# Attention scores from two float32r pieces in the two halves of the PE rows, and norm rows on GpSimd

## The reference, cut to what matters

```python
Q, K, V = split_heads(x @ q_w.T), split_heads(x @ k_w.T), split_heads(x @ v_w.T)   # 16 heads of 8
# per block of 64 keys: running maximum m, running sum l
scores = einsum('bhqd,bhkd->bhqk', Q, K_blk) * SCALE
m_new = maximum(m, scores.max(-1)); corr = exp(m - m_new); e = exp(scores - m_new)
l_new = e.sum(-1) * corr + e.sum(-1);  out_new = out * corr + e @ V_blk
out = (out / l) @ out_w.T + out_b
```

## Time and profile before

| | |
|---|---|
| median of 3 runs | 1854.68 us (1850.48 to 1855.77) |
| profiled execution | 1854.35 us, of which the span of its instructions is 1852.4 us |
| granted TensorE clock, mean | 0.944 |
| busy: PE, VectorE, ScalarE, GpSimd | 89%, 74%, 64%, 34% |
| attention pipeline | about 47 to 950 us of the span |

### The profile page before, as it was taken

How to read it: one execution, slowest core, us unless ns; L and a number is a source line. 1 busy time by engine, 2 the same in 40 slices (tenths; PEclk the granted TensorE clock), 3 DMA queues, 4 the chain that set the end, 5 groups by cost and what they waited for, 6 DMA issues and landing times. The chain is left out here.

```text
span 1852.4 us, 34677 instructions
## 1 busy us (share of the span) xinstructions
PE 1653.6 (89%) x8576; PEld 867.7 (47%) x8577; DVE 1367.3 (74%) x3309; ACT 1187.3 (64%) x2294; POOL 626.2 (34%) x965
## 2 busy tenths in 40 slices
PE   2899999999999999999969999999778884699996
PEld 1233333333333333333237777777545553366664
DVE  3899989999998999988655666666636774466665
ACT  1488888888888888888846666666425664244342
POOL 1213223232222322221122333333324776244444
PEclk7699999999999999999979999999988986799998
DMA  3333232222222222221010000000030112321220
GB/s 91 73 99 85 69 81 59 72 61 68 74 68 78 61 68 65 62 75 40 15 63 1 1 1 0 0 0 0 1 95 2 48 49 75 88 61 56 59 57 17
DMA packets 99517, 94.33 MB, mean 51 GB/s; under 512 B 15707, under 2 KB 93281, under 8 KB 99440
## 3 DMA queue, kind: packets, MB, share of 16 engines
q1 hardware_dynamic: 94064, 80.75, 16.7%
q0 software_dynamic: 5376, 12.66, 1.9%
HBM read 61.96 MB, written 31.14 MB: 50 GB/s over the span
## 5 line engine op out<-in xcount | busy, mean ns | idle before, releaser
L666 ACT ACTIVATE EX<-PS 128x512 f32<-128x512 f32 x1024 | 604.4, 601 | 150.2 <-PE PS L567 113.9
L816 DVE TENSOR_REDUCE bmax<-PS 128x16 f32<-128x1024 f32 x512 | 618.1, 1219 | 88.4 <-PE PS L555 80.4
L567 PE MATMUL PS<-QR,KR 75*128 75x512 bf16 x1024 | 392.1, 384 | 4.1 <-ACT EX L666 1.6
L555 PE MATMUL PS<-KR,QR 72*128 72x512 bf16 x1024 | 313.5, 388 | 39.7 <-DMA KR<-k_scr 22.6
L577 PE MATMUL PS<-EX,VS 128*9 128x512 f32 x2048 | 267.7, 595 | 2.5 <-ACT OT L672 1.6
L567 PEld LDWEIGHTS PS<-QR,KR 75*128 75x128 bf16 x1024 | 98.2, 96 | 329.9 <-ACT EX L666 273.6
L756 POOL TENSOR_TENSOR m_diff<-m_prev,m_all 128x16 f32<-128x16 f32 x64 | 14.2, 221 | 441.8 <-DVE m_all L828 441.8
L555 PEld LDWEIGHTS PS<-KR,QR 72*128 72x128 bf16 x1024 | 99.0, 99 | 124.9 <-issue 34.7
L1023 PE MATMUL PS<-pA,wb 128*128 128x512 f32 x640 | 156.8, 401 | 0.0
L1852 ACT ACTIVATE g<-PS 128x512 f32<-128x512 f32 x72 | 43.0, 597 | 142.3 <-PE PS L1812 142.3
L1023 PEld LDWEIGHTS PS<-pA,wb 128*128 128x128 f32 x640 | 120.0, 190 | 27.5
(11 more groups left out here) (230 smaller groups left out, 2857.4 us busy)
## 6 DMA issues: line engine op xcount, KB each, us to landing
QR<-q_scr SPq DMA_DIRECT2D x192, 96.0 KB
KR<-k_scr SPq DMA_DIRECT2D x192, 96.0 KB
rows<-row_scr SPq DMA_DIRECT2D x72, 129.0 KB, 2.1
q_scr<-partsB SPq DMA_DIRECT2D x70, 128.0 KB, 2.3
k_scr<-partsB SPq DMA_DIRECT2D x42, 128.0 KB, 2.3
X<-in_L_attn_x SPq DMA_DIRECT2D x16, 256.0 KB, 2.9
w_raw<-in_L_ffn_h_w SPq DMA_DIRECT2D x8, 256.0 KB, 3.0
q_scr<-parts SPq DMA_DIRECT2D x10, 128.0 KB, 2.4
```

What stands on the lines that cost most here:

```text
L555: mm = pe.matmul(PS[:, 2 * (pair % 2) + n % 2, :], QR[0:ROWS, i, h, t * P:(t + 1) * P], KR[0:ROWS, i, h, :], start=True, stop=True)
L567: pe.matmul(PS[:, 4 + n % 2, :], KR[:, j, h, kt * P:(kt + 1) * P], QR[:, j, h, :], start=True, stop=True).then_inc(st_done, 1)
L666: act.activation(EX[:, kt % 2, h, :], PS[:, 4 + n % 2, :], ACT.Exp, scale=SCALE).then_inc(ex_set, 1)
L816: dve.tensor_reduce(rows[:, 2 * v:2 * v + 2, t, :], PS[:, 2 * (u % 2):2 * (u % 2) + 2, :].rearrange("p h (b k) -> p h b k", k=BLK), AX_X, ...
```

## The change

- q and k are split into two pieces held as float32r (`NPART` = 2): the high one is written by ScalarE, the low one is the difference that VectorE takes straight from PSUM (`low`). `split` on GpSimd, `residB`, `qkf` and its ScalarE copy are gone. Scratch tensors are float32.
- One head now needs 32 rows (2 x 2 pieces x 8), a zero row, and for T two rows of maxima: 33 rows for s and 35 for T. Even heads of a group lie at rows 0 up, odd heads at rows 64 up (`HALF`), and QR and KR are 128 rows by two heads.
- T takes the heads in the order 1, 0, 3, 2 (`head_T`), so that consecutive score matmuls of TssT lie in alternate halves; ORDER is the same.
- Loads of a group are eight of 64 KB instead of six of 96 KB, the maxima two DMAs instead of one; a chunk's pieces are stored by two and three DMAs of 256 KB instead of five and three of 128 KB.
- The epsilon and the norm's rows go to GpSimd (`normed`). x is loaded a second time into a static buffer `xB`; the residual sum goes to `x3`, and a DMA (`store_x`) brings it back into X.
- The maxima are split in two pieces: three GpSimd instructions instead of five, and their transposition is float32.
- In the first block GpSimd sets QR to 0 and KR to -1 whole (two memsets of 128x4096 float32) ahead of its first power, VectorE's four memsets of KR and the third-piece step go.

```diff
-NPART = 3
-ROWS = NPART * NPART * HD
+NPART = 2
+ZROW = NPART * NPART * HD
+SROWS = ZROW + 1
+TROWS = SROWS + NPART
+HALF = 64
...
-        KR = sb("KR", [KROWS, NG, HG, S], BF16, att)
+        KR = sb("KR", [P, NG, 2, S], F32R, att)
+        QR = sb("QR", [P, NG, 2, S], F32R, att)
...
+                pool.memset(QR[:].bitcast(F32), 0.0).then_inc(kones, 1)
+                pool.memset(KR[:].bitcast(F32), -1.0).then_inc(kones, 1)
...
+        def head_T(n):
+            return (n % HG) ^ 1
...
-                    mm = pe.matmul(PS[:, 2 * (pair % 2) + n % 2, :], QR[0:ROWS, i, h, t * P:(t + 1) * P],
-                                   KR[0:ROWS, i, h, :], start=True, stop=True)
+                    rows = slice(HALF * (h % 2), HALF * (h % 2) + SROWS)
+                    mm = pe.matmul(PS[:, 2 * (pair % 2) + n % 2, :], QR[rows, i, h // 2, t * P:(t + 1) * P],
+                                   KR[rows, i, h // 2, :], start=True, stop=True)
...
-                    kt, h = n // HG, n % HG
+                    kt, h = n // HG, head_T(n)
+                    rows = slice(HALF * (h % 2), HALF * (h % 2) + TROWS)
-                    pe.matmul(PS[:, 4 + n % 2, :], KR[:, j, h, kt * P:(kt + 1) * P], QR[:, j, h, :],
+                    pe.matmul(PS[:, 4 + n % 2, :], KR[rows, j, h // 2, kt * P:(kt + 1) * P], QR[rows, j, h // 2, :],
...
-                        if some(n):
-                            act.wait_ge(split_B, n * 3)
-                        act.copy(qkf[:], bank).then_inc(use_read, 1)
...
+                def normed(b, ln, src, dst):
+                    rstd_eps(pool, b, ln)
+                    pool.wait_ge(ln["rstd"], b + 1)
                     settled(pool)
+                    for t in range(NT):
+                        pool.tensor_scalar(dst(t), src(t), ln["mv"][:, t, 0:1], ln["rs"][:, t:t + 1],
+                                           ALU.subtract, ALU.mult).then_inc(ln["steps"], 1)
...
+                def low(b, w):
+                    dve.wait_ge(part1_B, b * 2 + w + 1)
+                    dve.tensor_tensor(partsB[:, w, 1, :], PS[:, 7, :], partsB[:, w, 0, :],
+                                      ALU.subtract).then_inc(part2_B, 1)
+                    dve.wait_ge(part2_B, b * 2 + w + 1)
+                    dve.sem_inc(use_read, 1)
...
+                        if u == 2 and i >= 2 and exists(b + 2):
+                            low(b, i - 2)
```

More of the change, by code:

```diff
@@ L287, in _ @@
                 pool.wait_ge(ones_set, 3)
[L289 to L295, removed]
+                pool.memset(QR[:].bitcast(F32), 0.0).then_inc(kones, 1)
+                pool.memset(KR[:].bitcast(F32), -1.0).then_inc(kones, 1)
+                run_stages(pool, AHEAD, [(0, lambda c, s: rstd(ln1)(pool, c))])
             @block.vector
@@ L468, in _ @@
                 sp.dma_start(bias[:], io["L0_attn_out_b"].to_broadcast([P, P])).then_inc(w3_in, 16)
-                sp.wait_ge(kones, NG)
+                sp.wait_ge(kones, 2)
                 def load(b, i):
[L472 to L479, removed]
+                    for a in range(2):
+                        heads = slice(i * HG + a, (i + 1) * HG, 2)
+                        for r in range(2):
+                            rows = slice(HALF * a + r * NPART * HD, HALF * a + (r + 1) * NPART * HD)
+                            sp.dma_start(QR[rows, i].bitcast(F32), q_scr[ds(b, 1), heads]
+                                         .rearrange("b h j d t -> (j d) (b h) t")).then_inc(load_in[i], 16)
+                            sp.dma_start(KR[rows, i].bitcast(F32), k_scr[ds(b, 1), heads, r:r + NPART]
+                                         .rearrange("b h j d t -> (j d) (b h) t")).then_inc(load_in[i], 16)
@@ L481, in load_max @@
                 def load_max(i, g):
                     sp.wait_ge(mrow_set, g + 1)
-                    sp.dma_start(QR[ROWS:KROWS, i].rearrange("r h q -> r (h q)"),
-                                 m_row[:, i % 2, :]).then_inc(mrow_in[i % 2], 16)
+                    for a in range(2):
+                        rows = slice(HALF * a + SROWS, HALF * a + TROWS)
+                        sp.dma_start(QR[rows, i].rearrange("r h q -> r (h q)").bitcast(F32),
+                                     m_row[a * NT * HG:(a + 1) * NT * HG, i % 2, :]).then_inc(mrow_in[i % 2], 16)
@@ L503, in store_k @@
+                def store_q(d):
+                    sp.wait_ge(part2_B, (d - AHEAD) * 2 + 1)
                     settled(sp)
                     for j in range(NPART):
+                        sp.dma_start(q_scr[ds(d, 1), :, j].rearrange("b h d t -> (b h) d t"),
+                                     partsB[:, 0, j, :].bitcast(F32)).then_inc(q_out, 16)
+                def store_k(d):
+                    sp.wait_ge(part2_B, (d - AHEAD) * 2 + 2)
+                    settled(sp)
+                    for j in range(NPART + 1):
@@ L538, in step @@
                         (store_q, store_k)[i](b + 1)
+                    if i == 2 and exists(b - 2):
+                        store_x(b - 2)
                     if isinstance(g, int) and g < NWB:
                         load_weights(g)
-                run_groups(sp, step, 2)
+                run_groups(sp, step, TAIL)
+                sp.wait_ge(x3_out, NCH * 16)
             @block.tensor
@@ L661, in exps @@
                     act.wait_ge(st_done, g * 16 + n + 1)
[L662 to L664 removed]
+                    kt, h = n // HG, head_T(n)
+                    if n % HG == 0 and some(g * 4 + kt - 1):
                         act.wait_ge(pv_done, g * 4 + kt - 1)
@@ L780, in add_residual, with tiles @@
+                def tiles(buf):
+                    return lambda t: buf[:, t * P:(t + 1) * P]
                 def add_residual(c):
-                    pool.wait_ge(lnA["steps"], c * LN_STEPS + LN_STEPS)
-                    pool.tensor_tensor(chunk_of(X, c), chunk_of(X, c), y3[:], ALU.add).then_inc(x3_set, 1)
+                    pool.wait_ge(lnA["steps"], c * LN_SPLIT + LN_SPLIT)
+                    if some(c):
+                        pool.wait_ge(x3_out, c * 16)
+                    pool.tensor_tensor(x3[:], chunk_of(X, c), y3[:], ALU.add).then_inc(x3_set, 1)
```

185 lines of the change are left out of this document (72 added, 113 removed).

## The result

The median is 1834.92 us (1831.35 to 1862.71, four runs) against 1854.77 (1850.48 to 1855.77) for the kernel before: a ratio of 0.989 [0.988, 0.991]. 1781 was forecast. The direction is right and the time lies in the range of 1745 to 1840, but the gain is 20 us where 74 were expected. The ratio, here and in the experiments, leaves out runs over 1.5% above the fastest of the same kernel, here the one of 1862.71, whose granted clock was 0.917 where the others had 0.938 to 0.942. The profiled execution took 1831.35 us, 23.0 less than that of before.

A forecast was written before the change was run, and what follows sets the result against it. PE was taken as the bound, 52.7 of 54.2 us a chunk. After the change 49.2 a chunk, 1.25 less a group over 62 groups: 1854.35 - 77.5 + 4 for the edges = 1781 us, range 1745 to 1840.

The forecast's parts named there:

- no overlap: Rival for the score matmuls: row halves take turns, +4.0 us a chunk, 1920 us in all; chance 0.14.
- PE's need: PE's work per chunk of the attention pipeline: from 52.7 us to 42.1 with score pairs overlapping at 0.233.
- the 1.5 us loss of today: Attention pipeline: PE's waits per chunk before the change, 54.2 less 52.7, added to 47.7 to give 49.2.
- the T-to-exp time: Attention quarter: an exp starts 0.43 us after its T, read from the kernel before.
- The loop of 47.7: Attention pipeline: PE and ScalarE waiting in turn through order TssTv, 46.2 us a chunk, 47.7 with `copy_out`.
- the two changes round it: Bank 7's work: entering and leaving it changes the array's shape, 0.09 us each, +2.3 a chunk net.
- the coupled loop: Attention pipeline: order TssTv couples ScalarE and PE, 47.7 us a chunk; overlap with this loop had chance 0.65.
- the bounds of 46.7 and 52 a chunk: Limits on the attention period from the PE-ScalarE loop and VectorE's work, giving 1742 and 1824 us in all.
- 61 groups of 1.25: Attention pipeline: each group 1.25 us shorter, a quarter of 5.0 a chunk; the forecast counted 62, -77.5 us.
- the +2 of the forecast: Tail of the attention block: two norms in series on GpSimd and three T-only steps with more shape changes, +2 us.
- Weights bind: Rival for the score matmuls: each weight load takes the listed 0.19 us, -1.5 a chunk, 1835 us; chance 0.15.
- A lower clock: Part of the new-wait rival in the attention stage: PE's pauses lower the granted clock, 1855 to 1870 us; chance 0.06.

The follow-up runs named there:

- e2: Changed kernel with score matmuls over all 128 rows, so no halves (scores of two heads added, KR preset to -0.5): 1894.63 us, 1.020 of the kernel before.
- e3: Changed kernel with two bf16 pieces instead of float32r ones (scores less exact): 1795.16 us, 0.968 of the kernel before.
- e5: Changed kernel with ScalarE emptying bank 7 after the second exp of a quarter, not between first and second: 1848.49 us, 0.992 of the kernel before.
- e6: Changed kernel with bf16 pieces (scores less exact) and bank 7 emptied after the second exp: 1786.86 us, 0.962 of the kernel before.
- e9: Changed kernel with score matmuls reading 62 and 64 rows of a half instead of 33 and 35, same result: 1828.51 us, 0.987 of the kernel before.
- e14: Changed kernel, float32r, with 62 and 64 rows and all norm rows back on VectorE: 1833.88 us, 0.988 of the kernel before.
- e4: Changed kernel with the norms' rows back on VectorE, all else kept: 1849.85 us, 0.997 of the kernel before.
- e8: Changed kernel with bf16 pieces (scores less exact), bank 7 emptied after the second exp, norm rows on VectorE: 1833.12 us, 0.988 of the kernel before.
- e7: Changed kernel with all score matmuls in the lower row half (half of the heads' scores left out): 2717.86 us, 1.463 of the kernel before.
- e10: Changed kernel with all score matmuls in the lower half (half of the heads' scores left out), but 62 and 64 rows: 2702.5 us, one run.
- e11: Changed kernel with bf16 (scores less exact), bank 7 emptied later, 62 and 64 rows, last chunk's closing norm rows on VectorE: 1767.08 us, 0.954 of kernel before.
- e13: Changed kernel, float32r, with 62 and 64 rows, bank 7 emptied later, last chunk's norm rows on VectorE: 1822.68 us, 0.982 of the kernel before.
- e1: Changed kernel with T's heads in plain order, halves low, low, high, high: 1855.96 us, too scattered for a ratio; period 52.31.

## Why the prediction was off

**Right.** The halves overlap, T and s start within 0.01 us, so neither "no overlap" nor its 1920 came. v to T stayed 0.98. Nothing waits for the loads, stores or the maxima's DMAs. PE and ScalarE became coupled: their waits for each other head the list.

**The step that failed** is the size of PE's need and of the loop built on it: "PE's need becomes ... 42.1 a chunk" and, from it, "I add the 1.5 us loss of today: 49.2 a chunk". The sum put a float32r score pair at 0.233 always and a change of shape at 0.09 always, both right by themselves, and took the T-to-exp time from the bf16 kernel. Measured:

- After each change of shape the first float32r matmul holds up the next by 0.10 to 0.11 us (0.33 or 0.34 in place of 0.23), with full rows as with half rows (e2), and not with bf16 (e3). The fourth T of a quarter pays it without a change of shape too: where it comes late, having waited for its exp, bank 7's work starts 0.43 after it, as in the quarter shown; where it follows the s at once, 0.33; with bf16 mostly 0.32 either way. That its weight load is no longer hidden there is my reading; shown is that it goes with float32r and with a matmul that enters, after a change or a wait. (The Trainium skill, TensorE: Matmul & The Clock Gate, Part 2, LDWEIGHTS, has a load take its columns over 1.2 GHz; for 128 columns that is an estimate of 107 ns, and the 0.11 agrees with it, the listed 0.19 does not.) The stream of the earlier trace rows could not show it: 64 matmuls without a change of shape among them.
- The exp starts 0.61 after its T in the quarter shown, not 0.43. With bf16 it is 0.43.
- Together 16 x 0.19 = 3.0 us a chunk. With bf16 the period is 49.30, so these 3.0 are all but 0.1 of what the period missed of 49.2. That 49.30 and 49.2 lie so close is luck in part. The loop of 47.7 had no place for ScalarE's copy of bank 7 between the first and the second exp, which is worth 0.85 (e5) and 0.82 (e6), and the 1.5 us that were added were carried over from today's loss without a cause. With the copy out of the way 48.48 came.
- Bank 7's work, up to the next T: a turn 0.59 instead of 0.43, an output projection 1.09 instead of 0.89, the maxima 0.23 instead of 0.17. From a T on time to it: 0.33 instead of 0.22. Together a turn costs 0.26 more and a projection 0.31, where 0.18 was expected for the two changes round it. Seven turns, four projections and the maxima (0.08) make 3.4 a chunk in place of 2.3; with bf16 they cost nearly as much, so this is not the float32r price.
- Two slips in the working: the quarters sum to 32.0, not 32.2, and PE's need so to 41.9, which changes nothing, since the coupled loop was the longer term; and the bounds of 46.7 and 52 a chunk have no working.

**The rest of the sum**, against the profiled execution (50 us over the forecast): in the pipeline, between ScalarE's copies at 83.9 and 877.9 us, 28.2 were gained where 61 groups of 1.25 would be 76, hence +48. The first s came 2.8 earlier than forecast. The last two groups cost 7.9 more than before and the norms of the block's end 6.0, together 13.9 for the +2 of the forecast. The blocks behind, which the change does not touch, took 894.3 us in place of 900.2; in the other float32r runs with a profile they took from 897.2 (e9) to 905.7 (e14), so that this part moves by itself and the -6 is luck. The sum 48 - 3 + 12 - 6 is 51 of the 50.

**Rivals.** "Weights bind" named 1835, the time that came, but not by its mechanism: loads of the two halves do not queue at 0.19, since T and s start together, and a steady float32r stream is no slower than the earlier trace rows. The price comes only on entering, at about 0.11 and not at 0.19 a matmul. "A lower clock" came in part: 0.99 in most of the stage, but 0.51 for 14 us at its end, and single runs up to 1863. The argument against it, that PE would be over 80% busy, was worth nothing: the clock falls while PE is listed as 97 to 100% busy.

**The small terms.** A norm's rows on GpSimd cost 3.1, not 1.2; the bound had been 2.1 from a row with two inputs. Slack covered it in the pipeline (e4, e14), as was said, and not at the block's end. The memsets took 3.5 each, not 4.5, and the first s came earlier. VectorE's relief was worth nothing here, since it was not the bound; with bf16 pieces and late emptying it was worth 1.7 us a chunk (e8 against e6).

## What to carry to other kernels

When a matmul changes its type, take its price from rows where it stands between the neighbours that it will have: a steady stream hid about 0.1 us an entry, two entries a quarter, which ate 3 of the 5 us expected. A busy share of PE says nothing of its clock or of overlap; read the granted clock beside it, and follow starts. Work moved to an engine with slack is free in the steady state and to be paid where the pipeline ends.

## What the runs showed of the hardware

The granted clock fell to 1.2 GHz in kernels that use few rows of the array, with PE listed as busy 97 to 100%: for the whole stage with one half in use (e7, e10: 0.50), for stretches with 33 and 35 rows in both (0.51 for 14 us in the last groups after the change, 0.50 at the start of e5's profiled run), and not at the end of the stage with 62 and 64 rows, the added ones zero in QR (1.00 in e9). The profiled executions other than e7 and e10 divide without an exception. From the first to the last of ScalarE's copies the clock is 1.00 before the change, with full rows (e2) and with 62 and 64 rows (e9, e11, e13, e14). In the eight with 33 and 35 rows, float32r or bf16, it is 0.92 to 0.99. The spread between runs goes with it: 1831 to 1863 us with 33 and 35 rows, 1826 to 1831 with 62 and 64. What sets it stays open, since e10 has 64 rows and stays low. Matmuls in different row halves need not be adjacent or alternate to overlap (e1: T s s T with halves low, low, high, high is as fast, period 52.31 against 52.29).
